# Eight half-size regions for a chunked recurrence, two under way at a time

## The reference, cut to what matters

```python
Wx = einsum('bti,hi->bth', x, W)          # then normalised over the batch: gain and bias per channel
def step(yt, wx_t):
    yt = sigmoid(wx_t + yt @ V.T)
    return (yt, yt)
y0 = zeros((B, H))
_, ys = scan(step, y0, swapaxes(Wx, 0, 1))
t = t + ys                                 # the residual
```

## Time and profile before

| what | value |
|---|---|
| median of the three runs | 2014.13 us |
| the profiled execution, its own time | 2016.03 us |
| its span in the profile | 2014.2 us |
| mean granted TensorE clock, share of full speed | 0.888 |
| the stage of the recurrence in that span | from 764.8 to 1125.2 us |
| busy share over the whole span | PE 77%, DVE 73%, POOL 71%, ACT 63% |

### The profile page before, as it was taken

The page is one execution under the profiler, slowest core; times in us unless marked ns, Lnnn a source line. Parts: engine busy times, 40 slices in busy tenths (PEclk is TensorE's granted clock), DMA queues, the critical chain, the costliest instruction groups (busy, mean ns, idle before and its releaser), DMA issues. The chain is left out here.

```text
span 2014.2 us, 24846 instructions
## 1 busy us (share of the span) xinstructions
PE 1559.5 (77%) x5690; PEld 654.7 (33%) x5690; DVE 1472.8 (73%) x2369; ACT 1268.0 (63%) x2235; POOL 1435.8 (71%) x1066
## 2 busy tenths in 40 slices
PE   4999999999999962976681669999999999935200
PEld 1333333333333311654451332232332323204200
DVE  1789999999999862995686547999999999952000
ACT  3777777777777622975671348898888988820000
POOL 3999999999999940155685219988889888901571
PEclk8999999999999985987886789999999999965555
DMA  5578888888887658588986247878888887661011
GB/s 156 173 226 250 246 254 236 255 256 238 255 250 223 185 178 234 172 313 292 346 302 250 105 138 229 266 268 273 271 260 259 264 272 251 204 156 25 2 2 1
DMA packets 121185, 429.87 MB, mean 213 GB/s; under 512 B 53424, under 2 KB 58448, under 8 KB 75984
## 3 DMA queue, kind: packets, MB, share of 16 engines
q1 hardware_dynamic: 99360, 423.81, 66.7%
q10 hardware_dynamic: 18736, 4.29, 1.4%
q0 software_dynamic: 2944, 0.18, 0.1%
HBM read 257.91 MB, written 170.01 MB: 212 GB/s over the span
## 5 line engine op out<-in xcount | busy, mean ns | idle before, releaser
L454 ACT ACTIVATE tap_products<-xn,kk 128x512 f32<-128x512 f32 x384 | 275.3, 718 | 164.2 <-POOL x_and_products L485 159.8
L485 POOL TENSOR_TENSOR x_and_products<-tap_products,x_and_products 128x512 f32<-128x512 f32 x256 | 326.6, 1276 | 41.5 <-POOL x_and_products L485 3.5
L385 PE MATMUL pst<-xn,taps 128*128 128x512 f32 x768 | 351.1, 592 | 0.0
L1426 POOL TENSOR_SCALAR exp_q<-exp_q 128x512 f32<-128x512 f32 x128 | 201.6, 1575 | 118.7 <-ACT exp_q L1381 118.7
L896 DVE SCALAR_TENSOR_TENSOR pss<-region,bn,pss 128x256 f32<-128x256 f32 x432 | 194.4, 489 | 85.3 <-PE pss L798 84.4
L833 POOL TENSOR_TENSOR x_block<-x_block,region 128x2048 f32<-128x2048 f32 x24 | 133.1, 5545 | 148.0 <-ACT region L820 81.6
L543 DVE SCALAR_TENSOR_TENSOR pst<-xn,kk,pst 128x512 f32<-128x512 f32 x256 | 192.5, 752 | 62.0 <-PE pst L385 61.8
L385 PEld LDWEIGHTS pst<-xn,taps 128*128 128x128 f32 x768 | 145.6, 190 | 186.2 <-issue 186.2
L485 POOL TENSOR_TENSOR x_and_products<-tap_products,x_ring 128x512 f32<-128x512 f32 x128 | 164.2, 1283 | 19.3 <-ACT tap_products L454 19.3
L1440 POOL TENSOR_TENSOR q_z<-q_map,z_inv 128x512 f32<-128x512 f32 x128 | 163.7, 1279 | 7.1 <-issue 5.3
L425 ACT ACTIVATE sq<-x_ring 128x512 f32<-128x512 f32 x256 | 157.6, 622 | 16.7 <-POOL x_ring L492 10.1
(11 more groups left out here) (236 smaller groups left out, 3044.4 us busy)
## 6 DMA issues: line engine op xcount, KB each, us to landing
rstd_wide<-rstd_scratch SPq DMA_DIRECT2D x128, 512.0 KB, 7.2
x_ring<-in_x SPq DMA_DIRECT2D x32, 1024.0 KB, 5.3
x_scratch<-x_ring SPq DMA_DIRECT2D x32, 1024.0 KB, 4.3
xl_scratch<-wx SPq DMA_DIRECT2D x32, 1024.0 KB, 8.7
region<-xl_scratch SPq DMA_DIRECT2D x32, 1024.0 KB, 10.5
x_ring<-x_scratch SPq DMA_DIRECT2D x32, 1024.0 KB, 8.5
rstd_of_channels<-rstd_scratch SPq DMA_DIRECT2D x64, 512.0 KB, 6.0
x_transposed<-x_squares SPq DMA_DIRECT2D x64, 512.0 KB, 5.0
```

The costliest lines, as they stand in the source:

```text
L385: m = pe.matmul(wide(pst[g % 2]), taps[:, n * P:(n + 1) * P], tap_rows(g, t), start=(n == 0), stop=(n == len(PE_TAPS) - 1))
L454: act.activation(prod[:, n, :, :], tap_rows(g, t), ACT.Copy, scale=kk[:, t:t + 1]).then_inc(products, 1)
L485: pool.tensor_tensor(xr[:, g % XR, :], prod[:, n, :, :].rearrange("p r w -> p (r w)"), xr[:, g % XR, :] if n else x_tile(g), ALU.add).then ...
L1426: pool.tensor_scalar(e, e, 1.0, None, ALU.min).then_inc(clipped, 1)
```

## The change

The token line is cut into eight regions of 512 chunks (4 blocks each; `CLEN` stays 16, `STEPS` 28). A region now has two groups of 256 columns. Two regions are under way at a time: the program is written in slots, region r starts at slot 14 r, and in slot t the engines work the steps of the regions that are active, the older one first. There are 126 slots: in 98 of them four groups are in the ring, in the first 14 and the last 14 only two. Four region buffers of half size take the place of two, and four PSUM banks are used as before, two for each parity of r. `warm_state` gets a part for each parity. `x_block` has four slots in place of three, and the load of x1 (now three blocks ahead) is issued ahead of the load of the region's block. The bookkeeping on DVE stands at step 15 of each region, in one piece: one-column copy, subtraction and reduction for the region before, and then the copy into `reached`. The x1 blocks of the last region (four now) are loaded into the buffer of the fifth, region 4, while regions 5 and 6 run. At the end DVE makes the last check first and then adds blocks 0 and 2, POOL adds blocks 1 and 3.

```diff
-REGIONS = 4
+REGIONS = 8
-CHUNKS = 1024
+CHUNKS = 512
...
+        BUFS = 4
+        U = [sb(f"region{j}", [P, CLEN, 1 + CHUNKS], F32, regions) for j in range(BUFS)]
...
-            XSLOTS = 3
+            XSLOTS = 4
+            GROUPS = 2
+            HALF = STEPS // 2
+            SLOTS_B = HALF * (REGIONS + 1)
...
-            POOL_LAST = (2, 5)
+            POOL_LAST = (1, 3)
+            def active(t):
+                return [(r, t - HALF * r) for r in (t // HALF - 1, t // HALF) if 0 <= r < REGIONS]
...
# SP
                 for k in range(LAST):
                     r, i = divmod(k, RBLK)
                     store(k)
-                    if r + 2 < REGIONS:
+                    if k + XSLOTS - 1 < LAST:
+                        load_x1(k + XSLOTS - 1)
+                    if r + BUFS < REGIONS:
                         if i == 0:
                             sp.wait_ge(checked, r + 1)
-                            load_warm(r + 2)
+                            load_warm(r + BUFS)
                         if i == RBLK - 1:
-                            sp.wait_ge(kept, 1 + 2 * (r + 1))
-                        load_block(r + 2, i)
-                    if k + XSLOTS - 1 < LAST:
-                        load_x1(k + XSLOTS - 1)
+                            sp.wait_ge(kept, state_kept(r + 1))
+                        load_block(r + BUFS, i)
+                    elif r + BUFS == REGIONS and i == RBLK - 1:
+                        sp.wait_ge(checked, r + 1)
+                        sp.wait_ge(kept, state_kept(r + 1))
+                        for j in range(RBLK):
+                            sp.dma_start(last_x1(j), x1_d[LAST + j, :, :]).then_inc(last_x1_loaded, 16)
...
# DVE
-                for r in range(REGIONS):
-                    b = r % 2
-                    for s in range(1, STEPS):
+                for t in range(SLOTS_B):
+                    for r, s in active(t):
                         for j in range(GROUPS):
...
-                        if s == 3 and r:
-                            check_states(r - 1)
-                        if s == WARM + 1:
-                            keep_states(r)
+                        if s == HALF + 1:
+                            if r:
+                                keep_state(r)
+                                check_states(r - 1)
+                            keep_reached(r)
+                check_states(REGIONS - 1)
```

More of the change, by code:

```diff
@@ L684, in build_program @@
             LAST = NBLK - RBLK
-            POOL_LAST = (2, 5)
+            POOL_LAST = (1, 3)
+            def active(t):
+                return [(r, t - HALF * r) for r in (t // HALF - 1, t // HALF) if 0 <= r < REGIONS]
+            y_no, sum_no = {}, {}
+            for t in range(SLOTS_B):
+                for r, s in active(t):
+                    for j in range(GROUPS):
+                        y_no[r, s, j] = len(y_no) + 1
+                        if s:
+                            sum_no[r, s, j] = len(sum_no) + 1
@@ L749, in store @@
                     sp.dma_start(x2_d[k, :, :], xb[:, k % XSLOTS, :]).then_inc(x2_stored[k % XSLOTS], 16)
[L751 to L757, removed]
+                for r in range(BUFS):
+                    for i in range(RBLK):
+                        load_block(r, i)
+                    if r:
+                        load_warm(r)
+                    if r == BUFS - 2:
+                        for k in range(XSLOTS - 1):
+                            load_x1(k)
                 for k in range(LAST):
@@ L789, in _ @@
             def _(pe):
-                for r in range(REGIONS):
-                    b = r % 2
-                    for s in range(1, STEPS):
+                for t in range(SLOTS_B):
+                    for r, s in active(t):
                         for j in range(GROUPS):
-                            pe.wait_ge(y_ready, y_count(r * STEPS + s, j))
+                            if s == 0:
+                                continue
+                            pe.wait_ge(y_ready, y_no[r, s - 1, j])
                             if s == WARM and r == 0 and j == 0:
                                 pe.wait_ge(fixed, 1)
-                            before = ws_at(s - 1, j) if s <= WARM else step_cols(b, s - 1 - WARM, j)
-                            pe.matmul(pss[j][:, 0:GC], vT[:, :], before, start=True, stop=True).then_inc(carried, 1)
+                            before = ws_at(r, s - 1, j) if s <= WARM else step_cols(r, s - 1 - WARM, j)
+                            pe.matmul(ps_at(r, j), vT[:, :], before, start=True, stop=True).then_inc(carried, 1)
                 pe.wait_ge(checked, REGIONS)
@@ new lines, in _ @@
+                for t in range(SLOTS_B):
+                    for r, s in active(t):
+                        for j in range(GROUPS):
+                            if s == 0:
+                                wait_group(act, r, j)
+                                act.activation(ws_at(r, 0, j), warm_cols(r, 0, j), ACT.Sigmoid, bias=bias_w,
+                                               scale=gain_w).then_inc(y_ready, 1)
+                                continue
+                            act.wait_ge(summed, sum_no[r, s, j])
+                            if s % 2 == last_warm and s < WARM and r >= 2:
+                                act.wait_ge(kept, reached_kept(r - 2))
+                            if s >= WARM + CLEN - WARM and j + 1 < GROUPS:
+                                act.wait_ge(summed, sum_no[r, WARM - 1, j + 1])
+                            after = ws_at(r, s, j) if s < WARM else step_cols(r, s - WARM, j)
+                            act.activation(after, ps_at(r, j), ACT.Sigmoid, bias=bias_w).then_inc(y_ready, 1)
+                        if r == 0 and s == WARM - 1:
+                            act.wait_ge(y_ready, y_no[0, WARM - 1, 0])
+                            first = ws[:, 0, last_warm, 0:1]
+                            act.activation(first, first, ACT.Copy, scale=0.0).then_inc(fixed, 1)
@@ L886, in check_states @@
                         dve.sem_inc(checked, 1)
-                for r in range(REGIONS):
-                    b = r % 2
-                    for s in range(1, STEPS):
+                for t in range(SLOTS_B):
+                    for r, s in active(t):
                         for j in range(GROUPS):
-                            dve.wait_ge(carried, sum_count(r, s, j))
+                            if s == 0:
+                                continue
+                            dve.wait_ge(carried, sum_no[r, s, j])
```

123 lines of the change are left out of this document (51 added, 72 removed).

## The result

The changed kernel takes 1999.16 us (median of 4 runs, 1996.82 to 2001.08) against 2014.39 us for the kernel before on the same chip: a ratio of 0.9922, 95% interval 0.9905 to 0.9939. That is 15 us less, where 8 were forecast. In the profiled executions the spans are 2014.2 and 1994.4 us, and the whole difference lies in the stage of the recurrence, which is the row of the fence (busy time by stretch, all engines, as the earlier trace rows): 340.4 us for 360.4.

What follows compares the result with a forecast made beforehand. No engine is full: load waits, one group's way round, holds, DMA and tail bind in turn. Start -14.5 and tail -36, against half-empty slots and seven holds, gave -8 us: 2006 us (own range 1998 to 2016, for all 1978 to 2026).

Steps and rivals of the forecast that it cites:

- The holds: DVE's bookkeeping after each region waits for POOL's adds while the ring stands: 8.0 us each, seven holds.
- the full slots: Slots with four groups in the ring: 1.786 us each, 25.0 for 14, plus 2.9 for returning to full clock.
- the tail: From the ring's end to the next phase, last adds, keys and check: 22 us, against 58.4 before.
- the half-full slots: First and last 14 slots, two groups in the ring: PE at half clock, 2.32 us a turn.
- the sum: Whole stage: ring done at 1095.2 plus 22 gives 1117.2 against 1125.2, -8 us, so 2006 us.
- Start: Region 0 needs only two groups loaded, so the ring starts at 781.7 in place of 796.2: -14.5 us.
- First half region alone: Slots 0 to 13, two groups at half clock: 0.6 + 13 x 2.32 = 30.8 us, until 812.5.
- rival 1: In the half-full slots the clock comes back with two groups: -22 us, 1992 us; chance 0.17.
- DMA and POOL beside it: Per region, DMA's twelve transfers take 36.2 us and POOL 24, hidden if the period isn't much under 36.
- rival 2: DVE's copy precedes POOL's second add (or x1 is late): holds 3.0, DMA then decides, -41 us, 1973; chance 0.14.
- Last half region: End of the ring: two full-clock slots 3.6, hold 8.0, two groups with PE cold 27.8: 39.4 us, done 1095.2.
- Periods: Six region periods, slots 28 to 111, each 25.0 + 8.0 + 2.9 = 35.9 us: 215.4 us, to 1055.8.

Runs made afterwards that it cites:

- experiment 3: Changed kernel with its eight regions run one after the other, only two groups in the ring at any time: 2110.52 us.
- experiment 1: Changed kernel with DVE's bookkeeping one step later (step 16 in place of 15): 2029.38 us.
- experiment 2: Changed kernel without the copy into `reached`, warm states kept in three buffers in turn and subtracted in place: 1969.08 us.
- experiment 7: Changed kernel with ACT copying the warm states into two PSUM buffers, where DVE subtracts with one operand from PSUM: 1963.24 us.
- experiment 5: Changed kernel with three x1 slots and x1's load behind the region's load, as in the kernel before: 1983.86 us.
- experiment 9: Changed kernel with four x1 slots kept, but x1's load again behind the region's load: 1990.68 us.
- experiment 10: Changed kernel with three x1 slots, x1's load still ahead of the region's load: 1998.93 us.

## Why the prediction was half right

The holds, the full slots and the tail went as written, the half-full slots did not. The median, 1999.16 us, lies in the forecast's own range of 1998 to 2016, and that is luck: the range left 3 us for the clock, while the clock alone took 11.8 us off the sum, which by the trace comes to some 1994.

**Start: right.** The second group's step came at 781.88, 781.7 was forecast.

**First half region alone: wrong, and this is the step that failed.** The step was "I take half clock: 0.6 + 13 x 2.32". The clock rose after the first turn, and the part from 781.9 to the first region's last group went at 1.79 us a turn but for one fall: region 0's first add starts at 833.34, where the sum had the region done at 840.4, so ready for POOL at 839.9. That is 6.6 us of the 12 by which the sum missed the trace. The stretch of 8.2 us that decided it was a bad guide: it shows PE working with gaps at half clock, but other matmuls, in bursts with 0.9 to 1.3 us idle between them, and the ring behaves otherwise; what makes the difference no run shows. The Trainium skill, TensorE: Matmul & The Clock Gate (Part 1: The HAM clock gate), has it that matmul activity releases the throttle, whatever the number of matmuls; experiment 3 agrees, with a mean clock of 0.94 over 408 us of two groups. The stretch at 1780, at 0.50, doesn't. This was rival 1, given 0.17; its two terms were 9.8 and 4 us, measured are 6.6 and 5.2.

**The holds: right, all seven.** 1.1 of waiting, 0.68, then the copy behind the second add: forecast 1.8 and 5.3 us, measured 1.78 and 5.16. Periods 35.9 forecast, 35.7 measured. Experiments 1, 2 and 7 show that this is POOL's add and not the bookkeeping's own cost: the subtraction takes 5.9, 1.8 or 0.7 us according to when it comes and where its operands lie. The clock fell after each hold as forecast (0.50 over 916.5 to 922.0 in the changed kernel).

**DMA and POOL beside it: right as far as it was needed.** DMA's own 36.2 us were close to the period, and I called them hidden as long as the period was not much shorter; after the start no step of the ring waits for a block. Experiments 2 and 7 went under the period, and in 7 the ring met DMA as rival 2's working had it, though not at its times (ring end 1046 there; 1059 and 1035 measured in 2 and 7), and came out at 1969 and 1963 us where it said 1973.

**Last half region: the same error.** 39.4 us were forecast, from 1047.6 + 0.5 to 1082.3 it took 34.2: the hold cost what was said, but the clock came back by 1064.5.

**Tail: right.** 22 forecast, 23.0 measured. The last add of DVE ends 18.5 us after the ring, 18.3 forecast; from `flag` (1101.5) to the next phase it is then 3.8 in place of 2.0, and why is open.

Together: -6.6 (start of the ring), -1.1 (periods), -5.2 (end), +1.0 (tail) make the 11.9 us by which the traced stage, 340.5 us, lies under the forecast 352.4. The medians differ by 15.2 us, the two profiled executions by 19.2 (2016.03 and 1996.82 us); the changed kernel's runs lie up to 4.3 us apart and the profiled one is the fastest of them, 2.3 below the median, while the profiled execution before lies 1.6 above its own. So the trace overstates the gain, and the error of the sum, by some 4 us.

**What the prediction didn't ask.** It took x1's place in SP's queue as a help ("The x1 loads come first in the queue, so add two has its data") and saw that this puts the second add ahead of the copy, but it did not follow that this edit by itself makes the kernel slower. Experiments 5, 9 and 10 do: the change contains some 31 us of gain and a loss of 15. How much of the loss is the copies alone and how much that later subtractions fall into POOL's gaps was not separated.

## What to carry to other kernels

When two engines take turns at something, a stage's time depends on which of them comes first by a few tenths of a microsecond; write down who arrives when, for each of the two, before moving either, and prefer an edit that takes one of them away from the meeting (here the copy on ACT and `reached` in PSUM, 36 us) to one that shifts it. Feeding an engine earlier can make its neighbour wait. And a stall's price is read from what is behind it: the same edit was worth 3 us with four regions, where loads hid the stalls, and 36 with eight.

## What the runs showed of the hardware

DVE's subtraction with both operands in SBUF and its copy of 128x512 from SBUF to SBUF never ended inside a POOL add that was under way when they came, in any of the traces, and the one that waited went next: up to 5.96 us in place of 0.68, and up to 5.38 in place of 0.42. The copy of one column (128x1, 0.15 us at 873.59) was not held. The same subtraction with one operand and its result in PSUM took 0.69 us in the middle of an add; which of the two counts was not separated. TensorE at 1.2 GHz came back to 2.4 under a ring that leaves it idle for part of every turn (busy 12.66 of 17.00 us at a clock of 0.98), and fell again now and then for some microseconds (0.58 over 803.0 to 806.5) without a change in the work: the clock of such a stretch is not to be read from one other stretch.
